# A mixture-of-experts layer: GpSimd's and TensorE's programs for the 32 certain tiles written out, expert numbers loaded by fours

## What is computed

```python
xt = mix(x, cond).reshape(-1, 512)                 # 2048 rows
scores = softmax(xt @ router_w + router_b) + router_bias
# keep 2 of 4 groups of 4 experts, then the 2 best experts: gate[t, e]
for e in range(16):
    h = silu(xt @ w1[e] + b1[e]) * (xt @ w2[e] + b2[e])     # 512 -> 128
    y += gate[:, e:e+1] * (h @ w3[e] + b3[e])               # 128 -> 512
z = silu(xt @ sw1 + sb1) * (xt @ sw2 + sb2) @ sw3 + sb3     # shared, hidden 256
out = x + y + z
```

## Time and profile before

| | |
|---|---|
| runs | 282.87, 286.74, 289.75 us (median 286.74) |
| span of the profiled execution | 282.6 us; no other time is given for that execution, and the nearest run is 282.87 |
| busy | PE 90%, DVE 53%, POOL 45%, ACT 28% of the span |
| granted TensorE clock | 0.988 of full speed over the span |
| DMA instruction queues | 7 and 8 packets, 0.11 and 0.07 MB |

### The profile page before, as it was taken

One profiled execution on the slowest core, in us unless ns is written; L12 is line 12 of the kernel. 1 busy time (PEld: TensorE's weight loads), 2 busy tenths in 40 slices (PEclk: granted clock), 3 DMA queues, 4 the chain that ended last, 5 costly groups with the idle time before them and its releaser, 6 DMA issues.

```text
span 282.6 us, 4281 instructions
## 1 busy us (share of the span) xinstructions
PE 253.3 (90%) x1092; PEld 163.0 (58%) x1093; DVE 150.1 (53%) x314; ACT 78.6 (28%) x169; POOL 126.0 (45%) x204
## 2 busy tenths in 40 slices
PE   7959889899999859999999889889988979999975
PEld 6826667688864436677775455545555544444421
DVE  0497988569799763344333322332233130179894
ACT  2213455303164002333433232223322221000400
POOL 7673445310111456565656556565656565000160
PEclk9977999999999999999999999999999999999999
DMA  7996876882639359533443343434344433799963
GB/s 224 328 402 217 296 249 205 319 328 121 223 113 420 137 157 369 178 116 119 141 133 121 117 112 107 124 103 148 111 119 140 139 124 118 241 390 388 395 255 148
DMA packets 20699, 57.91 MB, mean 205 GB/s; under 512 B 2533, under 2 KB 2533, under 8 KB 20428
## 3 DMA queue, kind: packets, MB, share of 16 engines
q1 hardware_dynamic: 15084, 39.89, 39.2%
q0 software_dynamic: 5600, 17.83, 19.7%
HBM read 40.94 MB, written 17.30 MB: 206 GB/s over the span
## 4 chain that ended last, share of the span: by engine, by line
PE 38%; issue 26%; POOL 18%; DVE 12%; POOLq 3%; DMA 2%; ACT 0%
PE psum L560 36%; POOL late_region L486 12%; DVE r L959 3%; POOL from_slot L483 3%; DVE xT L1189 2%; POOL to_slot L493 2%; DVE xT L954 2%; DVE xT L928 2%; PE psum L603 2%; DVE xT L969 1%; POOL expert_rows L497 1%; DMA late_region<-xt_rows,from_slot 1%; DMA xT<-cond_pack 1%; DVE mix_bias L956 1%; POOLq L480 1%
## 5 line engine op out<-in xcount | busy, mean ns | idle before, releaser
L560 PE MATMUL psum<-wexp,r 128*128 x272 | 70.2, 387 | 2.1 <-issue 1.2
L560 PEld LDWEIGHTS psum<-wexp,r 128*128 128x128 f32 x272 | 47.1, 190 | 28.9 <-issue 22.8
L928 DVE TENSOR_TENSOR r<-psum,ebias 128x256 f32<-128x256 f32 x34 | 14.4, 425 | 82.5 <-PE psum L560 82.5
L486 POOL DMA_INDIRECT late_region<-xt_rows,from_slot x36 | 36.7, 1019 | 28.5 <-POOL from_slot L483 25.3
L497 POOL DMA_INDIRECT expert_rows<-late_region,to_slot x34 | 34.0, 1001 | 30.1 <-POOL to_slot L493 28.3
L560 PE MATMUL psum<-wexp,xt_sb 128*128 x68 | 36.7, 621 | 7.9 <-issue 7.9
L560 PE MATMUL psum<-xT,shared_sb 128*128 128x512 f32 x64 | 28.0, 593 | 0.8 <-issue 0.8
L871 ACT ACTIVATE late_region<-psum 128x512 f32<-128x512 f32 x34 | 20.3, 597 | 29.5 <-PE psum L560 29.5
L865 ACT ACTIVATE r<-r 128x128 f32<-128x128 f32 x34 | 10.5, 309 | 60.2 <-DVE r L928 60.2
L706 PE MATMUL psum<-ident,late_region 128*128 128x128 f32 x144 | 22.3, 277 | 3.6 <-DMA late_region<-xt_rows,from_slot 3.5
L1145 DVE COPY r<-psum 128x512 f32<-128x512 f32 x36 | 24.6, 684 | 1.5 <-PE psum L706 1.3
(11 more groups left out here) (175 smaller groups left out, 327.7 us busy)
## 6 DMA issues: line engine op xcount, KB each, us to landing
wexp<-expert_pack SPq DMA_DIRECT2D x16, 768.0 KB, 5.2
wexp<-expert_rows SPq DMA_DIRECT2D x8, 1024.0 KB, 13.0
xt_rows<-xt_sb SPq DMA_DIRECT2D x16, 256.0 KB, 2.5
x_early<-x SPq DMA_DIRECT2D x2, 1024.0 KB, 9.0
late_region<-x SPq DMA_DIRECT2D x2, 1024.0 KB, 13.7
ebias<-expert_bias SPq DMA_DIRECT2D x1, 2048.0 KB, 7.2
out_dram<-x_early SPq DMA_DIRECT2D x8, 256.0 KB, 9.8
shared_sb<-shared_pack SPq DMA_DIRECT2D x1, 1536.0 KB, 16.7
```

Of the source, the lines that this page charges most:

```text
L486: nc.gpsimd.indirect_dma_start(out=xg[:, slot, :], out_offset=None, in_=xt_dram[:, :], in_offset=bass.IndirectOffsetOnAxis(ap=from_slot[:, ...
L560: return nc.tensor.matmul(dst, lhsT, rhs, start=start, stop=stop)
L928: return nc.vector.tensor_tensor(dst, a, b, op)
```

## The change

GpSimd's steps up to 2 x SURE - 5 and its closing pairs 14 to 17 use the step number as a constant, so that the DMA takes its row numbers straight from the column of `from_row` or `to_row`; the copies and `hold` are gone there, and plain waits stand in their place. Only tiles from pair 18 on (not reached with 17 pairs) keep the copies, and the last scatter, whose tile number is a register.

TensorE's 32 certain steps are written out. The expert numbers come in fours: one load of 4 before step 0, and at steps 1, 5, ... 25 a load of the 4 numbers i+3 to i+6; each number serves the up and the down product. The three count registers are loaded together ahead of step 0. The pairs beyond (steps 32 and 33 here) read their numbers one at a time as before.

```diff
-            def gather(i, slot):
-                nc.gpsimd.tensor_copy(from_slot[:, slot:slot + 1], from_row[:, bass.ds(i, 1)]
-                                      ).then_inc(from_copied, 1)
-                hold(from_copied, i + 1)
-                nc.gpsimd.indirect_dma_start(
-                    out=xg[:, slot, :], out_offset=None, in_=xt_dram[:, :],
-                    in_offset=bass.IndirectOffsetOnAxis(ap=from_slot[:, slot:slot + 1].bitcast(U32), axis=0),
+            def gather_by(column, slot):
+                nc.gpsimd.indirect_dma_start(
+                    out=xg[:, slot, :], out_offset=None, in_=xt_dram[:, :],
+                    in_offset=bass.IndirectOffsetOnAxis(ap=column.bitcast(U32), axis=0),
                 ).then_inc(xg_loaded[slot], 16)
...
+            def gather(i):
+                gather_by(from_row[:, i:i + 1], i % RING)
+
+            def scatter(i):
+                pool.wait_ge(y_ready, i + 1)
+                scatter_by(to_row[:, i:i + 1], i % RING)
+
+            def gather_ahead(i):
+                pool.wait_ge(xgT_done, i + 3)
+                gather(i + 6)
+
+            def pool_step(i):
+                gather_ahead(i)
+                scatter(i - 1)
...
-            with pool.Fori(1, (SURE - 2) // 2) as j:
-                for q in range(2):
-                    pool_pair(j * 2 + q, q)
+            for i in range(1, 2 * (SURE - 2)):
+                pool_step(i)
...
-            scatter(tiles - 1, 1)
+            hold(y_ready, tiles)
+            nc.gpsimd.tensor_copy(to_slot[:, RING:RING + 1], to_row[:, bass.ds(tiles - 1, 1)]
+                                  ).then_inc(last_copied, 1)
+            pool.wait_ge(last_copied, 1)
+            scatter_by(to_slot[:, RING:RING + 1], 1)
...
-            def pe_step(i, b, slot, loaded):
+            def pe_step(i, b, slot, loaded, e, e_before):
                 n = i if isinstance(i, int) else 3
-                e = expert_of(i)
...
-                    down(1 - b, expert_of(i - 1), i, i - 2 if n >= 3 else None)
+                    down(1 - b, e_before, i, i - 2 if n >= 3 else None)
...
+            def experts_from(i):
+                _, values = nc.values_load_multi_w_load_instructions(
+                    tile_expert[0:1, i:i + RING], engines=[mybir.EngineType.PE], min_val=0, max_val=E - 1)
+                return values
...
             pairs = count_of(pe, N_PAIRS)
-            pe_pair(0, 0, 16)
             tiles = count_of(pe, N_TILES)
-            pe_pair(1, 1, 32)
             tiles_less_2 = count_of(pe, N_TILES_LESS_2)
-            with pe.Fori(1, SURE // 2) as j:
-                pe_pair(j * 2, 0, j * 16 + 16)
-                pe_pair(j * 2 + 1, 1, j * 16 + 32)
+            experts = [*experts_from(0)]
+            for i in range(2 * SURE):
+                if i % RING == 1 and i + RING - 1 < 2 * SURE:
+                    experts += experts_from(i + RING - 1)
+                pe_step(i, i % 2, (i + 2) % RING, 16 * ((i + 2) // RING + 1), experts[i], experts[i - 1])
```

More of the change, by code:

```diff
@@ L480, in hold, with scatter_by, gather_copied, scatter_copied @@
                 pool.sem_inc(pool_held, 1)
-            def gather(i, slot):
+            def gather_by(column, slot):
+                nc.gpsimd.indirect_dma_start(
+                    out=xg[:, slot, :], out_offset=None, in_=xt_dram[:, :],
+                    in_offset=bass.IndirectOffsetOnAxis(ap=column.bitcast(U32), axis=0),
+                ).then_inc(xg_loaded[slot], 16)
+            def scatter_by(column, slot):
+                nc.gpsimd.indirect_dma_start(
+                    out=y_dram[:, :],
+                    out_offset=bass.IndirectOffsetOnAxis(ap=column.bitcast(U32), axis=0),
+                    in_=y_sb[:, slot, :], in_offset=None, bounds_check=ASSIGN - 1, oob_is_err=False,
+                ).then_inc(scattered[slot], 16)
+            def gather(i):
[9 more added lines that the diff above has]
+                scatter(i - 1)
+            def gather_copied(i, slot):
+                hold(xgT_done, i - 3)
                 nc.gpsimd.tensor_copy(from_slot[:, slot:slot + 1], from_row[:, bass.ds(i, 1)]
                                       ).then_inc(from_copied, 1)
-                hold(from_copied, i + 1)
-                nc.gpsimd.indirect_dma_start(
-                    out=xg[:, slot, :], out_offset=None, in_=xt_dram[:, :],
-                    in_offset=bass.IndirectOffsetOnAxis(ap=from_slot[:, slot:slot + 1].bitcast(U32), axis=0),
-                ).then_inc(xg_loaded[slot], 16)
-            def scatter(i, slot):
+                hold(from_copied, i - (2 * FAR + 5))
+                gather_by(from_slot[:, slot:slot + 1], slot)
+            def scatter_copied(i, slot):
                 hold(y_ready, i + 1)
@@ L494, in scatter @@
                                       ).then_inc(to_copied, 1)
[L495 to L515, removed]
+                hold(to_copied, i - (2 * FAR - 2))
+                scatter_by(to_slot[:, slot:slot + 1], slot)
             for i in range(RING):
-                gather(i, i)
+                gather(i)
             pool.wait_ge(counts_ready, 1)
             pairs, tiles = count_of(pool, N_PAIRS), count_of(pool, N_TILES)
-            gather_ahead(-2, -2)
@@ L522, in _, with closing_pair @@
[L522 to L525, removed]
-            with pool.Fori(1, (SURE - 2) // 2) as j:
-                for q in range(2):
-                    pool_pair(j * 2 + q, q)
-            def closing_pair(p, q):
+            for i in (-2, -1, 0):
+                gather_ahead(i)
+            for i in range(1, 2 * (SURE - 2)):
+                pool_step(i)
+            def closing_pair(p):
                 with pool.If(pairs > p + 2):
-                    pool_pair(p, q)
+                    for u in range(2):
+                        pool_step(p * 2 + u)
@@ L532, in closing_pair, with closing_pair_copied @@
                 with pool.If(pairs < p + 3):
                     for u in range(2):
-                        scatter(p * 2 + u - 1, (2 * q + u - 1) % RING)
+                        scatter(p * 2 + u - 1)
+            def closing_pair_copied(p, q):
+                with pool.If(pairs > p + 2):
+                    for u in range(2):
+                        gather_copied(p * 2 + u + 6, (2 * q + u + 2) % RING)
+                        scatter_copied(p * 2 + u - 1, (2 * q + u - 1) % RING)
+                with pool.If(pairs < p + 3):
+                    for u in range(2):
+                        scatter_copied(p * 2 + u - 1, (2 * q + u - 1) % RING)
@@ L536, in _ @@
             for q in range(2):
[L537 removed]
+                closing_pair(SURE - 2 + q)
             for q in range(2):
                 with pool.If(pairs > SURE + q):
[L540 to L541 removed]
+                    closing_pair(SURE + q)
+            with pool.If(pairs > FAR):
                 with pool.Fori(1, (PAIRS - SURE) // 2) as j:
```

9 lines of the change are left out of this document (6 added, 3 removed).

## The result

The changed kernel takes 264.55 us (median of 4 runs, 263.53 to 267.89) against 285.28 us before: ratio 0.9334, 95% interval 0.9286 to 0.9383. The profiled execution has a span of 261.6 us and took 263.53 us; a run takes 1.9 us more than its span, so the trace of before stands for about 284.5 us.

A forecast was written before the change was run, and what follows sets the result against it. GpSimd's 4.08 us turn was taken to bound the expert stage. Last transposes: 108.97 + 103.5 + 3.2 + 0.45 = 216.1 us, 13.7 saved; with 52.8 after them the span is 268.9, plus 2 makes 271 us, range 265 to 278.

The forecast's parts named there:

- The idle time ahead of a DMA: GpSimd's turn without copies: 0.2 to 0.3 us of each idle time stays, giving a turn of about 2.5 us.
- the first rival: GpSimd's turn: nothing overlaps, it takes 3.68 us and GpSimd keeps leading; 274.5 us, chance 0.15.
- The rest, 52.8 us, left as it is: From the last transposes to the end: 52.8 us unchanged, hanging on the last result's scatter and the reload.
- The start, +2.2: Ahead of step 0: register loads and checks add 2.4 us, the first gather's lost copy takes off 0.2.
- Loads of four, 3.2: TensorE's steps: six loads of four show 0.53 us each, 3.2 us together, from 0.5 to 5.9.
- loads of four cost one load: TensorE's expert loads: four come for one load's time, loads show 0.5 us; 267.7 us, chance 0.17.
- The branch, 0.45: TensorE's steps 32 and 33 stay behind a branch with single loads, adding 0.45 us.
- 33 steps at 3.137: TensorE's steps up to the last transposes: 33 at 3.137 us each, 103.5 us together.
- The 2 us between span and run time: Added to the predicted span of 268.9 us: half of the 4.1 us the earlier trace lay under the median.
- The lower end of the range: 265 us: cheap loads, those before step 0 hidden too, and none of the added 2 us.
- The slower rival: Written-out code must be fetched, TensorE or GpSimd standing still for each packet: 24 us more, 295 us, chance 0.03.

The follow-up runs named there:

- GpSimd's part alone: GpSimd's steps written out without copies, TensorE's program as in the kernel before (loop, two single loads a step): 259.24 us, ratio 0.9194 to before.
- copies kept: Changed kernel, GpSimd's steps written out but with copy, wait and hold again ahead of every indirect DMA: 283.72 us, ratio 1.0021 to before.
- scatter copies: Changed kernel with the copy, its wait and hold again ahead of the scatters only: 266.13 us, median of two runs.
- fours with counts spread: Changed kernel, loads of four kept, the three count loads moved from ahead of step 0 to steps 4, 6 and 8: ratio 0.9149 to before.
- idle matmuls: Changed kernel with ten unread matmuls of the identity behind the transposes of tile 1: 264.96 us, two runs.
- TensorE's part alone: TensorE's 32 steps written out with loads of four, GpSimd's program as in the kernel before, loop and copies included: 286.5 us, ratio 1.0133.

## Why the prediction came out as it did

The direction and the reason were right. GpSimd's copies set the pace; without them TensorE's 3.137 us do, and both halves of the change, run alone, say so: 0.9194 and 1.0133. The idle time ahead of a DMA was taken as 0.2 to 0.3 us and is 0.30; the first rival (a turn of 3.68 us) didn't happen: 0.97 + 0.30 + 1.01 + 0.30 makes 2.58 for a turn that waits for nobody. The changed kernel has no such turn, as its scatters wait for ScalarE, but the parts were tested: with one copy kept the turn is 3.39 us, against 3.4 expected.

The size was off: 20.95 us of span saved, 13.7 forecast. By terms:

- *The rest, 52.8 us, left as it is*: this is the step that failed most. It measured 49.43, 3.3 us less. I had let it hang on the last result's scatter and the reload behind it. The chain of both traces goes another way, through TensorE's shared group, in which TensorE runs 26.62 us without a break, beginning 5.15 us after the last transposes before the change and 3.51 after it; neither the scatter nor the reload is on it (before, then changed):

```profile
234.97 26.62 PE psum L560 x62
```

```profile
215.72 26.62 PE psum L580 x62
```

So what delays the shared group delays the end. In the trace of before TensorE begins it 3.08 us after the last transposes, here 1.44 us. That is 1.64 us, and the end of the wait for the gather is enough for it: GpSimd's part alone, with the old program of TensorE, has 1.42. While the transposes wait, the old program's loads behind them lie open (with copies kept and the new program it is 2.07 us, so those loads are about 1.0 of the 3.08). I had called those loads a consequence of the wait in the steps, and had not followed them past the last one.

```profile
205.65 0.60 PE L726 MATMUL psum<-ident,late_region 128*128 128x128 f32 x4
...
207.07 1.96 PE L580 MATMUL psum<-xT,shared_sb 128*128 128x512 f32 x4
```

The other 1.7 us are luck, and no work of the change. Near the end VectorE adds group 2 in eight instructions while GpSimd does adds of its own, and TensorE's shared group needs VectorE's. In the timeline of before (us from the span's start, busy us, then the work, its count, and the idle time ahead) the shared group begins at 232.90, VectorE's eight take 7.56 us, and TensorE waits 2.11:

```profile
232.90 1.95 PE L560 MATMUL psum<-xT,shared_sb 128*128 128x512 f32 x4 [0.81 <-issue]
...
263.00 7.56 DVE L1189 SCALAR_TENSOR_TENSOR xT<-wexp,tops,xT 128x512 f32<-128x512 f32 x8
...
267.07 2.94 POOL L553 TENSOR_TENSOR xt_sb<-xt_sb,wexp 128x512 f32<-128x512 f32 x2 [27.47 <-ACT wexp L915]
...
271.43 1.95 PE L560 MATMUL psum<-shared_sb,late_region 128*128 128x512 f32 x4 [2.11 <-DVE xT L928]
```

In that of the changed kernel they take 5.51 us and TensorE waits for nothing; the two adds of VectorE that take long there, 3.38 us, come later:

```profile
243.75 5.51 DVE L1215 SCALAR_TENSOR_TENSOR xT<-wexp,tops,xT 128x512 f32<-128x512 f32 x8
...
248.83 2.79 POOL L573 TENSOR_TENSOR xt_sb<-xt_sb,wexp 128x512 f32<-128x512 f32 x2 [28.20 <-ACT wexp L941]
...
250.12 1.96 PE L580 MATMUL psum<-shared_sb,late_region 128*128 128x512 f32 x4
...
251.69 3.38 DVE L1215 SCALAR_TENSOR_TENSOR xt_sb<-wexp,tops,xt_sb 128x512 f32<-128x512 f32 x2
```

What differs is when GpSimd begins: 4.07 us after VectorE's first add, or 5.08. The traces of the other kernels keep to this order (begin of GpSimd's adds, duration of VectorE's eight, wait of TensorE): GpSimd's part alone 4.29, 6.53, 1.07; the same again 4.07, 7.56, 2.11; scatter copies 4.43, 6.53, 1.08; fours with counts spread 4.65, 6.53, 1.08; idle matmuls 4.66, 6.52, 1.07; all others 4.82 to 5.39, 5.50 or 5.51, none. So an add of VectorE that meets one of GpSimd's takes about 1 us longer; by line, of before (ns min/median/max):

```profile
L1189 DVE SCALAR_TENSOR_TENSOR xT<-wexp,tops,xT x8: 746/750/1793, 263.0 to 268.8; 128x512 f32<-128x512 f32 x8
```

The same kernel (GpSimd's part alone) has 1.07 in one run and 2.11 in another (stretches of 50.08 and 51.17 us), so it is the moment at which the two meet and no term of the change. That is read from traces; no experiment was made on it. With the 1.74 by which 51.17 lies over 49.43, and the 1.64, the 3.33 are there within 0.05.
- *The start, +2.2*: it is +0.60 from the table to the transposes of tile 2. The loads cost 2.16 us (9.45 to 11.61 with TensorE's part alone), 2.4 forecast. But the gathers without copies give 2.28 (9.45 to 7.17 with GpSimd's part alone), where I had put 0.2. I counted one copy's 0.2 us and not the idle time behind it, the very thing that I had found in the loop: the first gather begins 0.31 us after the table instead of 1.19, which is 0.88. That is not all. The first gather itself takes 1.94 us in the trace of before (1.95 in the others with copies at the gathers) and 1.20 in that of the changed kernel (1.19 or 1.20 in the others without); why, no run shows. And TensorE's wait for VectorE ahead of the first up product is 0.27 us with GpSimd's part alone, 0.84 before. What remains, 0.60, is the half clock: 2.42 us from the first up product to the transposes, 1.82 or 1.83 in the kernels without it. The lines are of before and of GpSimd's part alone:

```profile
96.69 1.94 POOL L486 DMA_INDIRECT late_region<-xt_rows,from_slot  x1 [0.94 <-POOL from_slot L483]
```

```profile
99.78 1.99 PE L580 MATMUL psum<-wexp,r 128*128 x8 [0.27 <-DVE r L1165]
```

- *Loads of four, 3.2*: 1.44 us for the six (3.34 to 3.43 us a step against 3.14), 0.24 each. The rival "loads of four cost one load" had the load right (0.333 us), and missed that four checks and their issue show a little: 0.24 instead of 0.08. "Runtime: NRT & Kernel Launch", section "Instruction fetch mechanics", of the Trainium skill, with its 200 ns a register even when many are loaded at once, doesn't fit a load of four from SBUF in 0.333 us. That unrolling such loads by four amortizes their floor, as the Trainium skill has it in "DMA: Bandwidth & Descriptors", section "Latency and other measured facts", fits, though the 0.333 us are under the floor given there.
- *The branch, 0.45*: steps 32 and 33 took 3.28 and 3.57 us, 0.57 over two plain ones.
- *33 steps at 3.137* held, but for 0.22 us in step 1, which is at half clock at first (3.36 us).
- 0.9 us came from ahead of the table, where nothing was changed.

These make 3.3 (the rest) + 1.6 (the start) + 1.4 (loads, branch and what is left of the steps: 17.3 measured, 15.9 forecast) + 0.9 = 7.2 of the missing 7.25 us. The 2 us between span and run time were right by luck: they were to be half of the 4.1 us by which the trace seemed to lie under the median, and every run lies 1.9 us over its span. The lower end of the range was mis-summed: cheap loads, those ahead of step 0 hidden as well, and none of the 2 us make 212.9 - 1.95 + 52.8 = 263.8 us, not 265.

The slower rival, fetching written-out code: the instruction queue of 7 packets became 11 (0.18 MB instead of 0.11, the section on queues of the profile's page), that of 8 became 9, and no step stood still for one.

```profile
q8 instruction: 11, 0.18, 0.3%
```

## What to carry to other kernels

When an engine waits for its own small instruction ahead of every large one, the price is not only the small one's 0.2 us but the longer idle time behind it, 0.79 or 0.89 us here instead of 0.30; two such in a turn of 4.08 us were 1.5 us. My reading is that the large one can't be prepared before its wait ends: the earlier trace rows have 0.52 us of issue right behind the copy. Before a second engine's program is rewritten along with the first, run each half alone: here the second half cost 3.9 us from the table to the end (3.7 in the second pair of traces) and gave nothing. Register loads were free where a step had sequencer time to spare (two expert numbers at odd steps, one count at even ones), and dear ahead of the first step or in a heap: spread them.

## What the runs showed of the hardware

A gather behind another indirect DMA starts 0.30 us after it ends; behind a copy that it waits for, 0.79 us (a scatter 0.79 to 0.89), and a scatter that waits for ScalarE started 0.80 us after ScalarE was done.

An add of VectorE that meets an add of GpSimd takes up to 1.79 us instead of 0.75 (eight of them 5.51, 6.53 or 7.56 us); a shift of 0.75 us between the engines, from 4.07 to 4.82, went from the longest to the shortest.

TensorE's granted clock fell to half (1.2 of 2.4 GHz) behind 2.41 idle us at step 0: the window from 105.20 to 108.60 us has a granted clock of 0.51. Four matmuls of the second up product take 1.70 us in it, against 1.03 in the earlier trace rows:

```profile
107.30 1.70 PE L580 MATMUL psum<-wexp,r 128*128 x4
```

With ten matmuls in the gap and 1.90 idle us left the clock stayed at 1.00, in one trace. The length of a gap alone doesn't settle it: in the trace of before 2.59 idle us stand ahead of the first transposes, and the granted clock is 1.00 in the windows from 101.10 to 107 us; with copies kept 2.70 us stand there, and the clock is 0.50 from 103 to 104 us.

```profile
101.10 0.63 PE L706 MATMUL psum<-ident,late_region 128*128 128x128 f32 x4 [2.59 <-DMA late_region<-xt_rows,from_slot]
```

"TensorE: Matmul & The Clock Gate" of the Trainium skill, section "What's actually happening", says that the default state is throttled and that activity releases it; the fall behind a gap and the return to 1.00, at 109 us while TensorE works, agree. A stretch at half clock lies ahead of the table too, of a length that differs from trace to trace (0.90 and 1.00 in the two windows shown); the row table came at 92.4 to 95.9 us in the ten traces of the table above, and at 99.55 us in the changed kernel's second trace.
